# Eight-column clearings behind the scatters of the last groups and blocks, and five groups finished two blocks later

## The chip, the core and the metric

The kernel runs on one NeuronCore of a Trainium2 chip. The metric is the time of one execution on the device in microseconds (us); the time of a kernel is the median of its runs. An execution has five engines that work side by side: TensorE (PE, matmuls), VectorE (DVE), ScalarE (ACT), GpSimd (POOL) and SyncE (SP), each with its own queue of instructions, tied together by semaphores. In this kernel SP issues nearly all plain transfers, and POOL issues the scatters, which write rows to places in DRAM that a table names.

## The reference

4096 rows (tokens) of 128 numbers go through two stages, each wrapped as `x + layernorm(f(layernorm(x)))`. The first `f` is causal linear attention with 16 heads. The second is a mixture of eight experts, each row sent to its best two, beside one shared expert:

```
shared = new_gelu(xf @ Wfc_s + bfc_s) @ Wproj_s + bproj_s
probs = jax.nn.softmax(xf @ Wr, axis=-1)
topk_p, topk_i = jax.lax.top_k(probs, TOP_K)          # 2 of 8
topk_p = topk_p / jnp.sum(topk_p, axis=-1, keepdims=True)
...
for e in range(N_EXPERTS):
    h = new_gelu(xf @ Wfc[e] + bfc[e]) @ Wproj[e] + bproj[e]
    routed = routed + h * gate[:, e:e + 1]
return (shared + routed)
```

All inputs and outputs are float32 with rows of 128; an expert has 512 hidden units.

## The kernel before

The rows are cut into eight groups of 512 (`NS` = 8, four tiles of 128 rows each). A first phase works the attention and the shared expert group by group and routes each row: POOL scatters a group's rows into one list per expert in DRAM (`scatters`, L708; eight scatters a group, one for each tile and choice). The second phase works the lists in `NB` = 39 blocks of 256 rows. It has a loop on each engine:

- SP (`load_block`, `load_weights`, `load_rows`) loads a block's packed weights into one of six buffers (`NBUF` = 6), after `blk_yr` says that the block six before has been read, and then the block's rows.
- PE (`rows_turned`, `first_layer`, `second_layer`) turns the rows of block b, does the first layer of block b-1 (36 matmuls, L1524 to L1526) and the second layer of block b-2 (16 matmuls, L1551, semaphore `blk_mm2`). The second layer waits for the gelu, the gelu for `blk_fc`, which PE raises behind a first layer.
- ACT rounds weights and rows (L1134, L1138), and applies the gelu (L1154).
- DVE takes the remainders (L2125, L2128) and moves the second layer's result to SBUF (`yb`, L2157; it waits for `blk_mm2` and for the scatter of the block six before).
- POOL (`scatter_block`, L831) writes the block's 256 result rows to their places in `results`, as two scatters (c = 0 and 1). The two groups of rows that are routed last (eight scatters each) go through the same queue: the last of group 6's stand behind block 1.

**The clearings.** `still()` (L693) is a POOL instruction that writes zeros to a tile `spare` that nobody reads. In the kernel before it covers 128 x 384 numbers, and stands behind the last four scatters of one group, behind every scatter of the last two, behind both scatters of blocks 0 to 11, and behind the first scatter only of blocks 12 to 26; from block 27 on there is none. With 59 clearings, POOL's order is fixed by the program.

**Finishing a group.** When all blocks that can hold a group's rows have been scattered (`READY`), SP reads the group's results back (`results_in`, 512 KB; `Y_AFTER` says after which block). DVE multiplies by the gates and adds (`gated`, L2072; `GATED_AT`, `MOMENTS_AT`) and takes the moments, POOL takes the roots of two groups at a time (`roots`; `ROOTS_AFTER`), ACT normalizes (`final_norm`, L1170; `NORM_AT`), DVE adds the residual (`normed`, L2102; `NORMED_AT`), and SP stores the group (`store`). These tables place each of these steps behind the work of a block. Behind the loops stand the rest of the groups, the stores and the last group, whose results SP reads (`y_part`, L532) once every scatter has landed.

Of the kernel before, what the change touches and what calls it, by code (L numbers as in the profile page):

```python
# [15 lines left out]
P = 128  # L16
# [25 lines left out]
def sandwich_kernel(nc, x, w_qkv, b_qkv, w_out, b_out, wfc_s, bfc_s, wproj_s, bproj_s, wr, wfc, bfc, wproj,  # L42
# [7 lines left out]
    NB = PAIRS // BLK + NE - 1  # L50
# [11 lines left out]
    NBUF = 6  # L62
# [6 lines left out]
    LATE_SEGS = NS * NE + 1  # L69
    READY = [max(EARLY + NE, 2 * STEP * (g + 1) // BLK + NE - 1) for g in range(NS)]  # L70
    assert READY[NS - 1] == NB
    Y_AFTER = {26: 0, 27: 1, 28: 2, 30: 3, 34: 4, 38: 5}
    SHARED_FROM = 24

    lists = nc.dram_tensor("expert_lists", [NE * LIST + SPARE * BLK, ROW], F32).ap()
# [3 lines left out]
    with ExitStack() as ctx:  # L79
# [158 lines left out]


        ON_PE = 2  # L240
        spare = sb("spare", [P, 3 * P])
        diag = vr[:].rearrange("p e t -> p (e t)")[:, 0:2 * ON_PE * P].rearrange("p (t k d) -> p t k d", t=ON_PE, k=2)
        HALVED = 3

# [303 lines left out]
        def _(pool):  # L548
# [131 lines left out]
                       channel_multiplier=1).then_inc(s["pads_ready"], 1)  # L680

            AT_END = 4
            PAIRED = 27
            SINGLE = 2 * NBUF

            stills = [0]

# [131 lines left out]
            def scatter_block(b, n, turn):  # L819
                if isinstance(b, int) and b == 2:  # L820
                    scatters(NS + 1, 0, 2 * TILES)
                last = isinstance(b, int) and b >= NB - HALVED
                if last:
                    pool.wait_ge(s["half_yr"], b + 1 - NB + HALVED)
                else:
                    pool.wait_ge(s["blk_yr"], b + 1)
                    alone(pool)
                for c in range(2):
                    if last and c:
                        pool.wait_ge(s["blk_yr"], b + 1)  # L830
                    g.indirect_dma_start(  # L831
                        out=results,
                        out_offset=bass.IndirectOffsetOnAxis(ap=yrow[n][:, c], axis=0),
                        in_=yb[n][:, c, :], in_offset=None).then_inc(blk_scat[n], 16)
                    if b < SINGLE or b < PAIRED and c == 0:
                        still()

            def roots(pair):
# [11 lines left out]
                pool.wait_ge(s["fin_pow"], 2 * pair + 2)  # L850
                g.tensor_tensor(shift[:, at], neg_mean[:, at], rstd[:, at], ALU.mult).then_inc(s["fin_shift"], 1)

            ROOTS_AFTER = {26: 0, 30: 1}

            def step(b, n, turn):

# [7 lines left out]
        def _(act):  # L864
# [301 lines left out]
            def final_norm(g, tiles=range(TILES)):  # L1166
# [5 lines left out]
                if TILES - 1 in tiles:  # L1172
                    ins.then_inc(s["fin_n"], 1)

            NORM_AT = {32: (0, (0, 1)), 33: (0, (2, 3)), 34: (1, (0, 1)), 35: (1, (2, 3)), 37: (2, (0, 1)),
                       38: (2, (2, 3)), 39: (3, (0, 1, 2, 3))}

            ENDS_FROM = 5

# [438 lines left out]
        def _(dve):  # L1618
# [487 lines left out]
                dve.wait_ge(s["fin_n"], g + 1)  # L2106
                residual(g)

            GATED_AT = {25: 0, 27: 1, 29: 2, 31: 3, 33: 4, 37: 5}
            MOMENTS_AT = {26: 0, 28: 1, 30: 2, 32: 3, 34: 4, 38: 5}  # L2110
            NORMED_AT = {35: 0, 36: 1}

            def step(b, n, turn):

# [65 lines left out]

            gated(6, 1)
            moments(6)
            normed(2)
            normed(3)

# [56 lines left out]
```

## Time and profile before

| | |
|---|---|
| median of 3 runs | 385.13 us (382.33 to 385.97) |
| the profiled execution | 381.27 us, its span 379.4 us |
| PE busy | 336.1 us, 89% of the span |
| POOL busy | 290.6 us (77%); scatters L831 78 x 1009 ns, L708 64 x 1005 ns, clearings L693 59 x 436 ns |
| DVE, ACT busy | 288.4 us, 256.8 us |
| granted PE clock | mean 0.967 of full speed |

The profile is of one execution. A busy share is an average over stages with different limits, so the argument has to be made in the stretch in question. Starts of matmuls are recorded, their ends are modelled; "remote" as the reason for a wait means that the profile has no event that explains it.

### The profile page before, as it was taken

To read this page: it belongs to the slowest core of one execution; us is meant where nothing else is said; L and a number is where in the kernel's file an instruction comes from. 1 tells how busy PE (TensorE), PEld (TensorE's weight loads), DVE (VectorE), ACT (ScalarE), POOL (GpSimd) and SP (SyncE) were. 2 spreads that over 40 slices of the span, in tenths; PEclk is the share of its full clock that TensorE was granted. 3 is DMA by queue.
4 is the path that set the end of the run, shared out by engine and by line. 5 is a ranking of instruction groups with operands and counts; after the bars stand their busy time and mean duration, and the time that the engine had idled before them with its cause. 6 is when DMAs were issued, how large, how long until landed. Compare 5 with 4: busy or idle time off the path is not lost.

```text
span 379.4 us, 8176 instructions
## 1 busy us (share of the span) xinstructions
PE 336.1 (89%) x2497; PEld 291.0 (77%) x2497; DVE 288.4 (76%) x688; ACT 256.8 (68%) x692; POOL 290.6 (77%) x393
## 2 busy tenths in 40 slices
PE   7869896999899898998799998999998699989891
PEld 3538485797786867877598898889997699989871
DVE  4998999799899999899966467745543359687667
ACT  3958874896896887867426884466552477587674
POOL 8778799478888687888778888888888667776640
PEclk9979997999999999999999999999998899999997
DMA  6576766566382606125059569979874589987417
GB/s 188 164 208 182 179 167 125 114 199 156 113 225 76 177 31 182 48 90 156 30 168 278 147 181 268 263 239 282 263 244 147 165 267 383 314 243 246 125 56 204
DMA packets 53522, 69.18 MB, mean 182 GB/s; under 512 B 6365, under 2 KB 37386, under 8 KB 53482
## 3 DMA queue, kind: packets, MB, share of 16 engines
q1 hardware_dynamic: 47556, 58.58, 54.5%
q0 software_dynamic: 4544, 9.35, 7.3%
q10 hardware_dynamic: 1382, 0.79, 0.8%
q8 instruction: 16, 0.26, 0.3%
q14 instruction: 24, 0.20, 0.2%
HBM read 40.06 MB, written 18.15 MB: 153 GB/s over the span
## 4 chain that ended last, share of the span: by engine, by line
PE 29%; DVE 16%; issue 8%; ACT 7%; POOL 7%; another core or an unknown queue 2%; DVEq 0%; ACTq 0%; POOLq 0%
PE bO L1551 8%; PE bS L1551 6%; POOL expert_lists L708 4%; DVE KV L1702 3%; ACT hs L1154 2%; PE bV L1526 2%; PE bV L1524 2%; PE bV L1525 2%; DVE KV L1693 1%; DVE Z L1710 1%; PE bO L1335 1%; DVE X L1625 1%; PE bA L1524 1%; DVE w_lo L2125 1%
## 5 line engine op out<-in xcount | busy, mean ns | idle before, releaser
L831 POOL DMA_INDIRECT expert_results<-yb,yrow x78 | 78.7, 1009 | 29.5 <-issue 19.3
L708 POOL DMA_INDIRECT expert_lists<-rows,pos x64 | 64.3, 1005 | 19.4 <-issue 17.2
L1702 DVE TENSOR_TENSOR_SCAN KV<-bS,KV 128x1024 f32<-128x1024 bf16 x32 | 72.7, 2276 | 0.3
L1335 PEld LDWEIGHTS bO<-wout_rot,Z 128*128 128x128 f32 x512 | 60.6, 192 | 8.4 <-POOL Z L790 5.1
L1335 PE MATMUL bO<-wout_rot,Z 128*128 128x128 f32 x512 | 63.2, 277 | 2.1 <-POOL Z L790 1.8
L2149 DVE COPY yrow<-xb 128x2 int32<-128x2 int32 x24 | 7.7, 321 | 42.3 <-remote 18.7
L1154 ACT ACTIVATE hs<-bV,KV 128x256 f32<-128x256 f32 x56 | 22.0, 477 | 18.9 <-PE bV L1526 10.4
L1551 PE MATMUL bO<-KV,hs 128*128 128x128 f32 x232 | 30.5, 286 | 3.7 <-ACT hs L1154 2.3
L1551 PEld LDWEIGHTS bO<-KV,hs 128*128 128x128 f32 x232 | 28.5, 199 | 5.1 <-ACT hs L1154 3.2
L1305 PE MATMUL bA<-w2s_sb,hs 128*128 128x128 f32 x224 | 28.8, 277 | 0.0
L734 POOL TENSOR_TENSOR KV<-shared,vr 128x1024 f32<-128x1024 f32 x10 | 23.6, 2363 | 5.7 <-ACT shared L995 5.4
L1305 PEld LDWEIGHTS bA<-w2s_sb,hs 128*128 128x128 f32 x224 | 27.3, 193 | 0.2
L1524 PE MATMUL bV<-x_lo,w_hi 128*128 128x256 f32 x80 | 24.2, 302 | 3.3 <-DVE x_lo L2128 1.6
L1551 PE MATMUL bS<-Z,hs 128*128 128x128 f32 x192 | 24.1, 280 | 2.5 <-ACT hs L1154 2.5
L1693 DVE TENSOR_TENSOR KV<-bV,vr 128x1024 f32<-128x1024 f32 x22 | 25.9, 1201 | 0.4 <-DMA vr<-vr 0.4
L693 POOL MEMSET spare<- 128x384 f32 x59 | 25.8, 436 | 0.0
L1551 PEld LDWEIGHTS bS<-Z,hs 128*128 128x128 f32 x192 | 23.0, 196 | 2.7 <-ACT hs L1154 2.7
L881 ACT ACTIVATE rows<-X,shift,rstd 128x128 f32<-128x128 f32 x32 | 13.2, 482 | 16.3 <-POOL shift L626 16.3
L1154 ACT ACTIVATE hs<-bA,Z 128x256 f32<-128x256 f32 x24 | 10.1, 473 | 19.7 <-PE bV L1526 7.3
L1526 PE MATMUL bV<-x_hi,w_lo 128*128 128x256 f32 x80 | 22.3, 279 | 0.2 <-issue 0.2
L1525 PE MATMUL bV<-x_hi,w_hi 128*128 128x256 f32 x80 | 22.3, 279 | 0.0
L1710 DVE TENSOR_TENSOR Z<-KV,bV 128x1024 f32<-128x1024 f32 (+1 forms) x22 | 21.1, 1010 | 0.0
(370 smaller groups left out, 995.9 us busy)
## 6 DMA issues: line engine op xcount, KB each, us to landing
KV<-packed_weights SPq DMA_DIRECT2D x21, 578.0 KB
Z<-packed_weights SPq DMA_DIRECT2D x18, 578.0 KB
xb<-expert_lists SPq DMA_DIRECT2D x39, 129.0 KB
vr<-vr SPq DMA_DIRECT2D x16, 224.0 KB, 2.5
shared<-expert_results SPq DMA_DIRECT2D x7, 512.0 KB
vr<-vr SPq DMA_DIRECT2D x16, 192.0 KB
vr<-vr SPq DMA_DIRECT2D x16, 160.0 KB
vr<-vr SPq DMA_DIRECT2D x16, 128.0 KB
```

Of the source, the lines that this page charges most:

```text
L693: g.memset(spare[:], 0.0).then_inc(s["stilled"], 1)
L708: g.indirect_dma_start(out=lists, out_offset=bass.IndirectOffsetOnAxis(ap=pos[:, m:m + 1], axis=0), in_=rows[:, m // TILES, m % TILES, :], ...
L831: g.indirect_dma_start(out=results, out_offset=bass.IndirectOffsetOnAxis(ap=yrow[n][:, c], axis=0), in_=yb[n][:, c, :], in_offset=None).th ...
L1154: ins = a.activation(hb[m % 2][:, c], blk_h[m % 2][c // 2][:, (c % 2) * BLK:(c % 2 + 1) * BLK], ACT.Gelu_apprx_tanh, bias=wb[m][:, B1_AT + ...
L1305: ins = t.matmul(bA[:, j * D:(j + 1) * D], hs[:, c, j * P:(j + 1) * P], w2s_sb[:, c], start=False, stop=True, skip_group_check=True)
L1335: ins = t.matmul(bO[:, j * D:(j + 1) * D], Z[:, d, j * P:(j + 1) * P], wout_rot[:, d], start=False, stop=True, skip_group_check=True)
L1524: t.matmul(h, w[0], x_lo[m % 2][:], start=True, stop=False)
L1525: t.matmul(h, w[0], x_hi[m % 2][:], start=False, stop=False)
L1526: ins = t.matmul(h, w[1], x_hi[m % 2][:], start=False, stop=True)
L1551: ins = t.matmul(bank_y[:, r * D:(r + 1) * D], hb[m % 2][:, c, r * P:(r + 1) * P], wb[m][:, HID + c * D:HID + (c + 1) * D], start=(c == 0 ...
L1693: v.tensor_tensor(KV[:, 2 * pair:2 * pair + 2], bK[:].unsqueeze(1).broadcast_to([P, 2, STEP]), vr[:, 2 * pair:2 * pair + 2], ALU.mult).the ...
L1702: v.tensor_tensor_scan(w, ps_keep, w, 0.0, ALU.mult, ALU.add).then_inc(s["kv_sum"], 1)
```

## The change

There are two. First, `spare` is 8 columns wide instead of 384, and a clearing now stands behind both scatters of every block up to 35 (all but the last three); the two constants that said where clearings thin out and end are gone. The scatters of the groups keep theirs. There are 92 clearings (20 behind scatters of groups and 72 behind those of blocks) where there were 59. Second, groups 0 to 3 are read back two or three blocks later, and the gating, the moments, the roots and the norms of groups 0 to 4 (gating and moments of 0 to 4, norms of 0 to 2) stand two blocks later, or one; the residual of group 1 stands behind the loop.

```
-    Y_AFTER = {26: 0, 27: 1, 28: 2, 30: 3, 34: 4, 38: 5}
+    Y_AFTER = {29: 0, 30: 1, 31: 2, 32: 3, 34: 4, 38: 5}
-        spare = sb("spare", [P, 3 * P])
+        spare = sb("spare", [P, 8])
-            PAIRED = 27
-            SINGLE = 2 * NBUF
-                    if b < SINGLE or b < PAIRED and c == 0:
+                    if b < NB - HALVED:
                         still()
-            ROOTS_AFTER = {26: 0, 30: 1}
+            ROOTS_AFTER = {28: 0, 32: 1}
-            NORM_AT = {32: (0, (0, 1)), 33: (0, (2, 3)), 34: (1, (0, 1)), 35: (1, (2, 3)), 37: (2, (0, 1)),
-                       38: (2, (2, 3)), 39: (3, (0, 1, 2, 3))}
+            NORM_AT = {34: (0, (0, 1)), 35: (0, (2, 3)), 36: (1, (0, 1)), 37: (1, (2, 3)), 38: (2, (0, 1, 2, 3)),
+                       39: (3, (0, 1, 2, 3))}
-            GATED_AT = {25: 0, 27: 1, 29: 2, 31: 3, 33: 4, 37: 5}
-            MOMENTS_AT = {26: 0, 28: 1, 30: 2, 32: 3, 34: 4, 38: 5}
-            NORMED_AT = {35: 0, 36: 1}
+            GATED_AT = {27: 0, 29: 1, 31: 2, 33: 3, 35: 4, 37: 5}
+            MOMENTS_AT = {28: 0, 30: 1, 32: 2, 34: 3, 36: 4, 38: 5}
+            NORMED_AT = {37: 0}
             moments(6)
+            normed(1)
             normed(2)
```

On POOL, at the scatters of blocks 12 to 14, the order before is this (L831 is a block's scatter, two to a block, from the buffer `yb` of the block's number modulo 6; L693 is the clearing):

```order
L831 DMA expert_results<-yb0,yrow0 12032x128
L693 MEMSET spare 128x384
L831 DMA expert_results<-yb0,yrow0 12032x128
L831 DMA expert_results<-yb1,yrow1 12032x128
L693 MEMSET spare 128x384
L831 DMA expert_results<-yb1,yrow1 12032x128
L831 DMA expert_results<-yb2,yrow2 12032x128
L693 MEMSET spare 128x384
```

The same place after the change:

```order
L829 DMA expert_results<-yb0,yrow0 12032x128
L691 MEMSET spare 128x8
L829 DMA expert_results<-yb0,yrow0 12032x128
L691 MEMSET spare 128x8
L829 DMA expert_results<-yb1,yrow1 12032x128
L691 MEMSET spare 128x8
L829 DMA expert_results<-yb1,yrow1 12032x128
L691 MEMSET spare 128x8
L829 DMA expert_results<-yb2,yrow2 12032x128
L691 MEMSET spare 128x8
```

Each scatter has its clearing now, and the clearing is 8 wide; before, from block 12 on, a block's second scatter and the next block's first stood side by side.

On ACT, from behind the gelu in block 36's step, the order before is this (L1154 is the gelu of a block, L1170 the norm of two tiles or four, L1134, L1138 and L1142 a block's roundings and row numbers):

```order
L1134 ACTIVATE w_hi<-KV 128x512
L1138 ACTIVATE x_hi<-bH 128x256
L1142 ACTIVATE yrow<-xb 128x2
L1154 ACTIVATE hs<-bV,KV 128x256 x4
L1170 ACTIVATE SH<-SH,shift,rstd 128x128 x2
L1134 ACTIVATE w_hi<-KV 128x512
L1138 ACTIVATE x_hi<-bT 128x256
L1142 ACTIVATE yrow<-xb 128x2
L1154 ACTIVATE hs<-bA,KV 128x256 x2
L1154 ACTIVATE hs<-bB,KV 128x256 x2
L1170 ACTIVATE SH<-SH,shift,rstd 128x128 x2
```

The same place after the change:

```order
L1168 ACTIVATE SH<-SH,shift,rstd 128x128 x2
L1132 ACTIVATE w_hi<-KV 128x512
L1136 ACTIVATE x_hi<-bH 128x256
L1140 ACTIVATE yrow<-xb 128x2
L1152 ACTIVATE hs<-bV,KV 128x256 x4
L1168 ACTIVATE SH<-SH,shift,rstd 128x128 x2
L1132 ACTIVATE w_hi<-KV 128x512
L1136 ACTIVATE x_hi<-bT 128x256
L1140 ACTIVATE yrow<-xb 128x2
L1152 ACTIVATE hs<-bA,KV 128x256 x2
L1152 ACTIVATE hs<-bB,KV 128x256 x2
L1168 ACTIVATE SH<-SH,shift,rstd 128x128 x4
```

Block 36's step has gained the norm of two tiles, and block 38's now has four tiles instead of two ahead of the last block's gelu; the steps of blocks 32 and 33, further ahead, have lost theirs.

## Rows read from the trace of the kernel before

**Rows 1.** The page's costliest groups: scatters of blocks, and clearings.
```profile
L831 POOL DMA_INDIRECT expert_results<-yb,yrow x78 | 78.7, 1009 | 29.5 <-issue 19.3
...
L693 POOL MEMSET spare<- 128x384 f32 x59 | 25.8, 436 | 0.0
```

**Rows 2.** Windows: stretch, length, each engine's busy us, granted clock, DMA share, GB/s.
```profile
257.00:277.00 20.00, 20.00 (x178) 20.00 (x177) 10.92 (x32) 12.22 (x30) 18.02 (x25) 1.00 0.89 269
280.00:298.00 18.00, 13.62 (x94) 12.22 (x92) 4.22 (x12) 5.29 (x14) 14.69 (x19) 0.91 0.55 169
```

**Rows 3.** Timeline of PE: start, us; second layers of blocks 17, 18, 21, 22, 35.
```profile
276.86 1.95 PE L1551 MATMUL bS<-Z,hs 128*128 128x128 f32 x16
...
280.28 1.95 PE L1551 MATMUL bO<-KV,hs 128*128 128x128 f32 x16
...
298.50 1.27 PE L1551 MATMUL bS<-Z,hs 128*128 128x128 f32 x9 [2.48 <-ACT hs L1154]
...
303.62 1.95 PE L1551 MATMUL bO<-Z,hs 128*128 128x128 f32 x16
...
350.79 1.95 PE L1551 MATMUL bS<-Z,hs 128*128 128x128 f32 x16
```

**Rows 4.** Timeline of POOL: start, us, in brackets the idle time before it.
```profile
223.87 0.97 POOL L831 DMA_INDIRECT expert_results<-yb,yrow  x1 [0.16 <-issue]
...
278.00 0.96 POOL L831 DMA_INDIRECT expert_results<-yb,yrow  x1 [0.30 <-issue]
...
299.70 0.97 POOL L831 DMA_INDIRECT expert_results<-yb,yrow  x1 [2.19 <-DVE yb L2157]
```

**Rows 5.** Timeline of all engines: who waits between 283 and 292.
```profile
283.58 0.28 PE L1526 MATMUL bV<-x_hi,w_lo 128*128 128x256 f32 x1
...
287.50 1.57 ACT L1154 ACTIVATE hs<-bV,KV 128x256 f32<-128x256 f32 x4 [4.93 <-remote]
...
291.13 0.17 DVE L2149 COPY yrow<-xb 128x2 int32<-128x2 int32 x1 [5.56 <-remote]
```

**Rows 6.** The same in the first phase: the last of four scatters, then ACT.
```profile
94.05 0.96 POOL L708 DMA_INDIRECT expert_lists<-rows,pos  x1 [0.31 <-issue]
...
95.83 0.60 ACT L1030 ACTIVATE SH<-bA 128x512 f32<-128x512 f32 x1 [3.13 <-remote]
```

**Rows 7.** The same behind block 27, where no clearing stands.
```profile
330.25 0.96 POOL L831 DMA_INDIRECT expert_results<-yb,yrow  x1 [0.31 <-issue]
...
331.80 0.42 DVE L2157 TENSOR_TENSOR yb<-bS,Z 128x256 f32<-128x256 f32 x1 [2.36 <-remote]
...
335.98 0.96 POOL L831 DMA_INDIRECT expert_results<-yb,yrow  x1 [0.60 <-issue]
...
336.63 0.47 ACT L1154 ACTIVATE hs<-bV,KV 128x256 f32<-128x256 f32 x1 [1.21 <-issue]
```

**Rows 8.** POOL's instructions by form: a clearing of the setup, busy us, mean ns.
```profile
L580 POOL MEMSET eps<- 1x1 bf16 x3 | 0.3, 94 | 0.0
```

**Rows 9.** Timelines of ACT and POOL: last sum and roots before the last groups' rows.
```profile
209.98 0.19 ACT L934 ACTIVATION_READ_ACCUMULATOR shared<-X,neg_mean_scaled 128x1 f32 x1
...
210.94 0.22 POOL L622 TENSOR_TENSOR ve<-sq,ln_eps 128x4 f32<-128x4 f32 x1
```

**Rows 10.** The page: SP's reads of a group's results, KB each.
```profile
shared<-expert_results SPq DMA_DIRECT2D x7, 512.0 KB
```

**Rows 11.** Timelines of the tail: ACT ahead of the last gelu, SP, DVE.
```profile
358.65 0.89 ACT L1170 ACTIVATE SH<-SH,shift,rstd 128x128 f32<-128x128 f32 x2
...
367.79 2.22 SPq L532 DMA_DIRECT2D shared<-expert_results  x4
369.32 0.23 DVE L2187 RECIPROCAL rstd<-ve 128x12 f32<-128x12 f32 x1 [1.75 <-ACT ve L1195]
```

**Rows 12.** Timeline of DVE: the results of blocks 3 and 10.
```profile
227.33 0.61 DVE L2157 TENSOR_TENSOR yb<-bS,Z 128x256 f32<-128x256 f32 x1
...
255.84 0.42 DVE L2157 TENSOR_TENSOR yb<-bO,Z 128x256 f32<-128x256 f32 x1
```

## The prediction

> **What bounds the kernel now.** The page's costliest groups come first, for the size of what is changed: 78 scatters of blocks at 1009 ns and 59 clearings at 436 ns [rows 1]. POOL is busy for 77% of the span and PE for 89%, so what the clearings are worth has to be read where PE waits. The windows show two kinds of stretch [rows 2]. In 257 to 277, with a wide clearing at every block, PE is busy for 20.00 of 20 us. In 280 to 298 it is busy for 13.62 of 18, its granted clock falls from 1.00 to 0.91, and DVE and ACT do less than half as much (4.22 and 5.29 us): nobody works much, so there something is late for all of them.
>
> The timeline of PE gives the size. Second layers start at 276.86 and 280.28, a pace of 3.42 us a block; blocks 18 to 22 go from 280.28 to 303.62, 23.34 us where four blocks at that pace take 13.68 [rows 3]. So 9.7 us are lost there. From 22 to 35 it is 47.17 us for thirteen blocks, against 44.46 at that pace: 2.7 us more.
>
> The timeline of POOL shows what is particular to the place. In the kernel before, the clearings thin out at block 12, and POOL, which is behind with its scatters, works them off without a pause. A scatter that stands beside another starts 0.30 us behind it [rows 4], where a clearing of 0.44 with its issue makes the gap about 0.60. POOL has caught up at 299.70, where for the first time it waits for a result (`yb`). That is also where PE resumes. The timeline of all engines says how they are held: PE has finished a first layer at 283.58 + 0.28 = 283.86, but ACT, which waits for nothing else, starts its gelu at 287.50 after 4.93 us of a wait that is put down to "remote" (no event explains it), and DVE comes back only at 291.13 after 5.56 us [rows 5]. A run of four scatters in the first phase did it too: the last one ends at 94.05 + 0.96 = 95.01 and ACT, idle for 3.13 us, goes on at 95.83 [rows 6]. And behind block 27, where there is no clearing: scatter over at 331.21, DVE's sum at 331.80 after 2.36 us [rows 7]. I read this as one mechanism: while POOL issues scatters close together, news from PE reaches the others late, mostly in a bunch after the last of them. It costs 9.7 us in one run of scatters, and pieces of a microsecond or two behind block 27.
>
> **The change, part by part.**
>
> *The clearings behind blocks 12 to 35.* 33 more than before, on an engine that is waited for only in its long run. If a clearing of 8 columns does what the wide one does, the stretch of blocks 18 to 22 runs like 257 to 277 [rows 2], and its 9.7 us go (−9.7). Of the 2.7 behind block 22, some belongs to other causes, since also with wide clearings not every wait is gone; I take −2.0.
>
> *The width.* A clearing of 1 x 1 took 94 ns [rows 8] and the wide one, 384 columns, 436 ns [rows 1]; 128 x 8 has to lie between. By columns it is next to the first, and I take 0.11. So a clearing falls from 0.44 to 0.11, and the period of POOL's run from about 1.6 us to 0.97 + 0.11 + 0.17 = 1.25 a scatter. POOL is not what PE waits for in the second phase as long as it has six buffers in hand, so that is worth nothing by itself there. At the passage between the phases it is on the path: five clearings stand in POOL's run ahead of the roots of the last group, which start at 210.94, and 5 x 0.33 = 1.7 us would be the most. But ACT hands over the last sum at 209.98 + 0.19 = 210.17 [rows 9], so at most 0.77 can be gained; I take −0.5 (bounds 0 and −0.8).
>
> *Finishing later.* The reads of groups 0 to 3, 512 KB each [rows 10], now come behind blocks 29 to 32 in succession, ahead of the loads of blocks some six further on; a late load there has that lead to hide in, so 0 (if the lead were gone, a read would cost its own time, at most some 2 us). The gating, moments and roots only change places within the loops, equal work, 0. ACT's norms are not hidden: the norm of two tiles at 358.65 takes 0.89 us ahead of the last gelus [rows 11], about 0.77 of it not overlapped with its neighbours, and there is one such pair more in block 36's step and one more in block 38's, where ACT is next to PE in the chain that ends last: +1.5 (bounds 0, if ACT waits there anyway, and +1.8). DVE's residual of group 1 moves behind the loop, 0.66 us into idle time of 1.75 us that it has before 369.32 [rows 11]: 0. SP's store of group 1 moves with it, ahead of the last reads of results; four of those take 2.22 us to issue [rows 11], 0.55 each, and a store of one or two issues delays them by 0.55 to 1.1: +0.8.
>
> *The sum*: −9.7 − 2.0 − 0.5 + 1.5 + 0.8 = −9.9, made against the profiled execution's own 381.27, which gives 371.4. That execution is 3.9 us below the median of 385.13, so on the median it is 375.2: 375.
>
> **What speaks against it.** One row weighs on the step that all of this rests on. With a clearing 8 wide the gap between two scatters is 0.11 + 0.17 = 0.28 us. That is no longer than the 0.30 that stands between two scatters with nothing between them [rows 4], and those are the ones that hold PE's news back. The pause that is known to let it through is 0.60 long. Behind block 27 there is even a row for a pause of 0.60 without a clearing: the scatter at 335.98 stands 0.60 behind its neighbour, and ACT's gelu at 336.63 waited for nothing but its issue [rows 7]. What acts may therefore be the length of the pause, not that something else was executed.
>
> The Trainium skill bears on this in the GPSIMD Engine Reference, section 2.1 (Instruction dispatch): consecutive Pool instructions are no barrier between the engine's eight cores; each starts on the next instruction as soon as its own share is done. In DMA: Bandwidth & Descriptors, section SWDGE vs HWDGE vs iDMA, it says that two of those cores compute a scatter's descriptors and write them to rings in SBUF. By these two, a narrow clearing is for the two cores in question only a very short break and no fence, which speaks for the length of the pause; no row here shows the cores apart. By that rule the time would be the one that rival B gives from rows; if the clearing as an instruction is what lets the news through, it is the one above.
>
> **The rivals.**
>
> *B, the narrow clearing does not work like the wide one (slower).* Its place is the whole run of scatters from the last groups on. POOL's gaps there are then 0.28 instead of 0.60, from about 203 on, and the mechanism that now costs 9.7 us in 280 to 298 holds in the early blocks. The price of a block in it: 280.28 to 298.50 for three blocks, 6.07 us instead of 3.42, +2.65 [rows 3]. How long it would last: POOL's first scatter of a block is at 223.87 [rows 4]; eleven clearings ahead of it are 0.33 shorter, so it starts near 220.2; up to block 10 there are 30 scatters at 1.24, which end at 257.4, and block 10's result is there at 255.84 [rows 12]. So POOL catches up near 257 rather than near 299.70. In the 37 us up to there some 6 blocks would be done at 6.07, and the loss is 6 x 2.65 = 16, less what this stretch loses already: results of blocks 3 to 10 come from 227.33 to 255.84 [rows 12], 4.07 us a block, 0.65 x 7 = 4.6. That leaves +11.3, and +1 for the last groups. Against it the late stall goes, −9.7, and the tail and the passage stay as above, +2.3 − 0.5 (nothing off for the lags behind block 27, which B leaves). Sum +4.4: 385.7 of its own, 390 on the median. At half the price of a block the stretch costs 8 − 4.6 = 3.4 and the sum is −3.5, 382 on the median. I take 387, nearer to the whole price, and 380 to 396 as its bounds. It decides between 0.30 (holds) and 0.60 (passes) of gap.
>
> *C, the stall goes, but the end gives it back.* With POOL and PE earlier by 10 us, reads, norms and loads of blocks 29 to 38 meet in a stretch where SP moves a load and a read of 512 KB in every block. If the six-block lead is used up there and the norms are all on the path, some 6 us of the 12 come back: 381 on the median.
>
> *D, the scatters are not the cause.* Then the 9.7 us come from something else in 280 to 298 (transfers have a share of 0.55 there against 0.89 ahead of it [rows 2], so not from their mass), the change moves it elsewhere, and the tail's +2.3 remain: 385 to 387.5. The three places [rows 5 to 7] have nothing else in common than scatters side by side, so I hold it for unlikely.
>
> **How the numbers follow.** The forecast 0.5: every stretch with clearings between the scatters keeps PE running, and the change gives that to the places that had none. B 0.3: its gap speaks for it and only a size of clearing, not its presence, is changed in the first half. C 0.1, D 0.1. The forecast alone spans 370 to 379: the tail at its bounds (−2.3, or +1 and the read's 2), the run of the medians 382 to 386 around its own. To leave out 2 in 10 the range has to reach through C and D and into the lower half of B: 368 to 390. A difference of 1%, 3.9 us, is about what a measurement of this kernel can tell from no change. Faster by more than 1% (below 381.3): the forecast nearly whole, half of C, a little of B: 0.58. Slower by more than 1% (above 389.0): the upper part of B, 0.20 with some of D. The rest, 0.22, lies within.
>
> **What the next profile would show.** Right: clearings at 100 to 150 ns, no wait of over 3 us on "remote" on ACT or DVE, PE's second layers 3.4 to 3.5 us apart from block 3 to 35, its granted clock near 1.00 in 280 to 298, POOL's first wait for `yb` near block 10, at about 257. If B is right, that wait still comes near there, but PE is busy for only two thirds of 220 to 257, with ACT and DVE on "remote" waits. The steps of the tail show as the starts of ACT's norms around block 38, and as the issue of the last reads behind a store. What would make it wrong: the gap of 0.28 acting like 0.30 (B), or a price of the late stall that does not vanish when its scatters are set apart.

## The result, and the profile after

The changed kernel takes 394.08 us (median of 4, 393.25 to 396.69), the kernel before 385.29 in the same job (382.33 to 385.97). The ratio is 1.027, with an interval of 1.023 to 1.031: slower by 2.7%. The profiled execution took 394.43, its span is 392.6 us against 379.4. I had forecast 375, and given rival B, which ends slower, a chance of 0.3.

Where the 13.2 us of span went is read off the starts of PE's second layers (L1549 of the changed kernel is L1551 of the one before):

| from, to | before, us | after, us | difference |
|---|---|---|---|
| start to block 0 | 211.67 | 213.19 | +1.5 |
| block 0 to 7 | 29.75 | 46.82 | +17.1 |
| block 7 to 17 | 35.44 | 36.64 | +1.2 |
| block 17 to 22 | 26.76 | 18.81 | −8.0 |
| block 22 to 35 | 47.17 | 48.41 | +1.2 |
| block 35 to the end | 28.6 | 28.7 | +0.1 |

The stall behind block 18 [rows 2, 3] is gone almost in full, and twice as much has come up in the first seven blocks. Windows of the changed kernel (the stretch, its length, then busy us of PE, PEld, DVE, ACT and POOL, granted clock, share of the DMA engines, GB/s):

```profile
203.00:220.00 17.00, 14.59 (x129) 14.00 (x130) 8.72 (x28) 11.63 (x33) 11.83 (x22) 1.00 0.56 176
220.00:260.00 40.00, 24.52 (x186) 22.97 (x185) 16.05 (x72) 13.42 (x29) 25.23 (x47) 0.83 0.49 134
280.00:298.00 18.00, 16.42 (x145) 16.22 (x144) 8.74 (x24) 8.34 (x21) 11.30 (x22) 1.00 0.80 243
```

The same windows of the kernel before, of which only the last is in [rows 2]:

```profile
203.00:220.00 17.00, 15.48 (x138) 14.97 (x138) 9.61 (x38) 11.95 (x33) 15.33 (x22) 1.00 0.66 198
220.00:260.00 40.00, 36.84 (x330) 35.57 (x328) 26.01 (x91) 23.72 (x54) 35.86 (x52) 1.00 0.88 245
```

In 220 to 260 PE is busy for 24.5 of 40 us instead of 36.8, and its granted clock falls to 0.83. In 280 to 298 it is busy for 16.4 where it was for 13.6. The timelines of the changed kernel show who waits, and for what, from 217 to 231:

```profile
218.91 0.96 PE L1351 MATMUL bS<-wr_sb,xt 128*128 128x8 f32 x8
...
221.27 0.28 PE L1524 MATMUL bB<-x_hi,w_lo 128*128 128x256 f32 x1
229.37 0.21 PE L1359 MATMUL bS<-chosen,before 128*128 128x32 bf16 x1 [7.82 <-DVE chosen L1748]
...
217.08 0.42 DVE L2126 TENSOR_TENSOR x_lo<-bH,x_hi 128x256 fp32r<-128x256 f32 x1
227.09 0.19 DVE L1713 COPY lg<-bS 128x32 f32<-128x32 f32 x1 [9.59 <-remote]
...
219.59 0.66 ACT L1132 ACTIVATE w_hi<-Z 128x512 fp32r<-128x512 f32 x1
227.26 0.84 ACT L1152 ACTIVATE hs<-bA,Z 128x256 f32<-128x256 f32 x2 [7.02 <-remote]
```

PE has finished its first layer at 221.27 + 0.28 = 221.55; the gelu that waits for it starts at 227.26, 5.7 us later. DVE waits from 217.50 on for the router's product of PE, which PE finishes at 219.87, and takes it up at 227.09, 7.2 us later. POOL's timeline has a run of nine scatters at the same time, the last of which ends at 225.62:

```profile
213.83 1.41 POOL L706 DMA_INDIRECT expert_lists<-rows,pos  x1 [0.17 <-issue]
215.24 0.12 POOL L691 MEMSET spare<- 128x8 f32 x1
...
223.38 0.97 POOL L829 DMA_INDIRECT expert_results<-yb,yrow  x1 [0.18 <-issue]
224.34 0.13 POOL L691 MEMSET spare<- 128x8 f32 x1
224.66 0.96 POOL L829 DMA_INDIRECT expert_results<-yb,yrow  x1 [0.19 <-issue]
225.62 0.12 POOL L691 MEMSET spare<- 128x8 f32 x1
230.51 0.97 POOL L829 DMA_INDIRECT expert_results<-yb,yrow  x1 [4.77 <-DVE yb L2155]
```

A scatter, a clearing of 0.12 and 0.18 of issue: a period of 1.27 us and a pause of 0.31, with the news released behind the last of the run. That is the pattern of [rows 4, 5] at another place. The hold is not there from the first scatter on: the run begins at 213.83, and ACT still starts a gelu at 218.16, 1.3 us behind the first layer that it waits for, with other work in between. A second run of twelve, 230.51 to 245.45, is two scatters of block 1, the eight of the last group (group 7, and not group 6 as the description of the kernel before says) and two of block 2. DVE goes on behind it at 247.87, after 12.31 us on "remote"; the second layer that it waits for had ended at 235.24 + 1.95 = 237.19.

PE itself is held as well, which the word "news" does not cover. In the second layer below the program has a wait only ahead of the first of 16 matmuls, and yet they come one or a few at a time, and the profile has no event for the gaps ("issue"):

```profile
235.24 1.95 PE L1549 MATMUL bS<-Z,hs 128*128 128x128 f32 x16
...
242.24 0.77 PE L1549 MATMUL bO<-Z,hs 128*128 128x128 f32 x3 [2.78 <-issue]
244.89 0.37 PE L1549 MATMUL bO<-Z,hs 128*128 128x128 f32 x1 [1.88 <-issue]
246.35 0.37 PE L1549 MATMUL bO<-Z,hs 128*128 128x128 f32 x1 [1.08 <-issue]
247.75 2.51 PE L1549 MATMUL bO<-Z,hs 128*128 128x128 f32 x11 [1.03 <-issue]
```

The traces therefore do not tell a signal that comes late from engines that are themselves held up. Below, "held news" is the name of the pattern and not of a shown mechanism.

### The profile page after: what moved, and what is told of

The parts are those of the page before. It is cut to its first block, busy times and chain, and to the rows that moved or that the text cites. A ratio compares the mean times of both kernels' runs of the same rounds, so it can differ in the third digit from the quotient of the medians.

```text
span 392.6 us, 8202 instructions
## 1 busy us (share of the span) xinstructions
PE 335.2 (85%) x2490; PEld 291.4 (74%) x2497; DVE 288.7 (74%) x688; ACT 256.5 (65%) x692; POOL 278.0 (71%) x426
## 4 chain that ended last, share of the span: by engine, by line
PE 36%; POOL 15%; ACT 15%; issue 11%; DVE 8%; another core or an unknown queue 7%; SPq 3%; DMA 3%; POOLq 1%; DVEq 0%; ACTq 0%
PE bS L1549 7%; PE bO L1333 7%; PE bO L1549 6%; POOL expert_lists L706 3%; ACT hs L1152 3%; ACT hs L1023 2%; POOL Z L788 2%; PE bV L1522 2%; DVE SH L2070 2%; ACT shared L894 2%; POOL Z L793 2%; PE bV L1523 2%; PE bV L1524 2%; DMA shared<-expert_results 1%
## 5 line engine op out<-in xcount | busy, mean ns | idle before, releaser
L829 POOL DMA_INDIRECT expert_results<-yb,yrow x78 | 79.8, 1023 | 52.8 <-DVE yb L2155 33.4
L2147 DVE COPY yrow<-xb 128x2 int32<-128x2 int32 x24 | 4.5, 189 | 45.4 <-remote 22.1
L1549 PE MATMUL bO<-KV,hs 128*128 128x128 f32 x232 | 31.0, 289 | 4.6 <-ACT hs L1152 4.4
L1549 PEld LDWEIGHTS bO<-KV,hs 128*128 128x128 f32 x232 | 28.8, 201 | 6.0 <-ACT hs L1152 6.0
L732 POOL TENSOR_TENSOR KV<-shared,vr 128x1024 f32<-128x1024 f32 x10 | 23.6, 2362 | 5.7 <-ACT shared L993 4.6
L1549 PE MATMUL bS<-Z,hs 128*128 128x128 f32 x192 | 23.5, 275 | 0.2 <-ACT hs L1152 0.2
L879 ACT ACTIVATE rows<-X,shift,rstd 128x128 f32<-128x128 f32 x32 | 13.2, 482 | 15.4 <-POOL shift L626 15.3
L1549 PEld LDWEIGHTS bS<-Z,hs 128*128 128x128 f32 x192 | 22.4, 192 | 0.4 <-ACT hs L1152 0.4
L1708 DVE TENSOR_TENSOR Z<-KV,bV 128x1024 f32<-128x1024 f32 (+1 forms) x22 | 21.1, 1011 | 0.0
L1549 PE MATMUL bO<-Z,hs 128*128 128x128 f32 x96 | 13.8, 294 | 6.8 <-issue 6.8
```

The lines of the kernel that those rows point to most:

```text
L732: g.tensor_tensor(KV[:, 2 * pair:2 * pair + 2], keys.unsqueeze(1).broadcast_to([P, 2, STEP]), vr[:, 2 * pair:2 * pair + 2], ALU.mult).then ...
L829: g.indirect_dma_start(out=results, out_offset=bass.IndirectOffsetOnAxis(ap=yrow[n][:, c], axis=0), in_=yb[n][:, c, :], in_offset=None).th ...
L1549: ins = t.matmul(bank_y[:, r * D:(r + 1) * D], hb[m % 2][:, c, r * P:(r + 1) * P], wb[m][:, HID + c * D:HID + (c + 1) * D], start=(c == 0 ...
```

## The experiments

A job is one session on one chip, in which some kernels and the kernel before are run. All runs stand against the kernel before in the same job. **That kernel itself turned out to take 374 us in three of the eight jobs and 380 to 385 in five**, and the two kinds of job differ in the traces. I call them free and held. This is the table of all 18 runs, by job:

| job (chip) | before | kernel | median | ratio (interval) |
|---|---|---|---|---|
| 1 (4), free | 374.47 | e1 narrow alone | 365.51 | 0.975 (0.969 to 0.980) |
| | | e2 later alone | 369.50 | 0.987 (0.983 to 0.991) |
| | | e3 wide everywhere | 381.58 | 1.019 (1.015 to 1.023) |
| | | e4 none | 366.96 | 0.981 (0.974 to 0.987) |
| 2 (8), held | 384.72 | e5 changed | 396.15 | 1.030 (1.028 to 1.033) |
| | | e6 before, one run | 383.21 | |
| 3 (6), free | 374.12 | e7 narrow alone | 363.93 | 0.972 (0.969 to 0.976) |
| | | e8 later alone | 368.27 | 0.984 (0.982 to 0.987) |
| | | e9 none | 364.92 | 0.975 (0.970 to 0.980) |
| | | e10 three narrow | 397.03 | 1.060 (1.057 to 1.063) |
| 4 (6), held | 383.71 | e11 changed | 394.38 | 1.026 (1.018 to 1.034) |
| | | e12 narrow alone | 396.18 | 1.029 (1.020 to 1.038) |
| | | e13 wide, later | 379.83 | 0.991 (0.988 to 0.994) |
| 5 (9), held | 384.07 | e14 three narrow | 398.44 | 1.038 (1.033 to 1.044) |
| | | e15 changed | 398.38 | 1.034 (1.029 to 1.040) |
| 6 (7), free | 374.21 | e16 two narrow, later | 381.35 | 1.021 (1.016 to 1.026) |
| | | e17 none | 364.33 | 0.973 (0.969 to 0.976) |
| 7 (14), held | 380.11 | e18 changed | 391.68 | 1.029 (1.022 to 1.037) |

The job of the result above (held) is the eighth.

**The two parts alone, wide clearings everywhere, and none (job 1).** The edits, each on the kernel before: e1 takes over the clearings of the change, e2 its tables, and e3 and e4 are (shortened)

```
e3:  -  if b < SINGLE or b < PAIRED and c == 0:
     +  if b < NB - HALVED:                      (spare stays 128 x 384)
e4:  -  if in_passage(i, first): still()
     -  if b < SINGLE or b < PAIRED and c == 0: still()
```

> The kernel before with the changed clearings alone: 8 columns wide, behind every scatter up to block 35; the groups are finished where they were before. Theory (the pause between scatters decides, and 0.31 us is too short): the loss sits here, 220 to 257 runs with PE busy for two thirds only, and the time is that of the changed kernel less the tail's share of at most 2 us: 391 to 394 us. Rival (the later finishing costs the 9 us, the clearings are neutral or help): 376 to 386 us.

> The kernel before with the later finishing alone: clearings as before, 384 wide and thinned out from block 12. Theory: the stretch 203 to 300 is as before, with its stall of about 9.7 us in 280 to 298, and the tail gives +2.3 (two norms ahead of the last gelus 1.5, a store ahead of the last reads 0.8): 386 to 389 us. Rival (the later finishing is what made it slower): 392 us or more. A third, from the reads of results being better placed: 381 to 384.

> The kernel before with its clearings of 384 columns, but behind both scatters of every block up to 35; the groups finished as before. Theory (a pause of 0.6 us between scatters lets the news of PE through): the stall of 280 to 298 goes (-9.7) and the lags behind block 27 in part (-2), none of the rest changes: 372 to 377 us. Rival (the late stall has another cause, or POOL with the longer period falls behind and becomes what is waited for): 382 to 388 us.

> The kernel before without any clearing, so scatters stand 0.30 us apart throughout; the groups finished as before. Theory (only the length of the pause counts): like the narrow clearings, 391 to 394 us, with the same two waits of about 10 us of DVE in 216 to 248. Rival (a clearing of any width does something by being there): the stalls of the early blocks are longer than with narrow ones, 397 us or more.

Neither theory nor rival had this, but for e3, where the rival (POOL falls behind) came close. Narrow clearings alone gained 2.5%, none at all gained 1.9%, the later finishing gained 1.3%, wide ones everywhere lost 1.9%. And the kernel before took 374.5. The trace of e2, which has the clearings of the kernel before, shows why these four can't be held against the verdict. On POOL, bare scatters stand 0.30 apart from block 12 on as in [rows 4], and PE's second layers of blocks 18 to 21 come 3.41 to 3.42 us apart all the same:

```profile
275.96 0.95 POOL L831 DMA_INDIRECT expert_results<-yb,yrow  x1 [0.30 <-issue]
276.90 0.44 POOL L693 MEMSET spare<- 128x384 f32 x1
277.51 0.96 POOL L831 DMA_INDIRECT expert_results<-yb,yrow  x1 [0.17 <-DVE yb L2157]
278.78 0.95 POOL L831 DMA_INDIRECT expert_results<-yb,yrow  x1 [0.30 <-issue]
...
278.25 1.95 PE L1551 MATMUL bO<-KV,hs 128*128 128x128 f32 x16
281.66 1.95 PE L1551 MATMUL bS<-KV,hs 128*128 128x128 f32 x16
285.08 1.95 PE L1551 MATMUL bO<-KV,hs 128*128 128x128 f32 x16
288.50 1.95 PE L1551 MATMUL bS<-Z,hs 128*128 128x128 f32 x16
```

No wait in these four traces is put down to "remote". There was no held news in this job, so what is left to see is the price of POOL's lateness. The waits of SP in e3 (engine and line, what it waited for: us in total, times, longest):

```profile
SPq L508 <- DMA expert_results<-yb,yrow: 36.1, 3, 13.9
```

and of PE:

```profile
PE bH L1377 <- DMA xb<-expert_lists: 10.0, 2, 9.7
```

Behind the loads of block 26 SP waits for the scatters up to block 20 (`READY` of group 0 is 21) before it reads group 0's results back; the loads of later blocks stand behind it in its queue, and PE runs out of blocks for 9.7 us. In e1, with the shorter period, the waits of L508 are 20.7 us, in e2, with the later read, 8.4. So in a free job both parts of the change relieve the same wait, and wide clearings only cost. Narrow ones cost nothing that can be told from none at all (0.975 against 0.981). There is no trace of the kernel before from a free job, so how much of either gain comes out of this wait is argued and not shown.

**The changed kernel and the one before again (job 2).**

> The changed kernel itself, once more. In the four runs ahead of this one the kernel before took 374.5 us, not 385.3, and no trace of them has a wait on remote on ACT or DVE, not even the one without any clearing, where the trace of the changed kernel has 34 us of them on ACT and 35 on DVE. Theory (the held back news of PE depends on the chip that the kernel runs on, and where it is absent the narrow clearings cost nothing and the later finishing gains): if this runs on a chip that does not hold it back, 361 to 366 us against 374.5, with no remote waits; on one that does, 393 to 396 against 385. Rival (narrow clearings and later finishing together make the stalls, on any chip): 2 to 3% slower than the kernel before here too, with DVE waits of about 10 us in 216 to 248.

> The kernel before itself, for a trace on this chip. Theory: where it takes 374 to 375 us, its trace has no waits on remote, and 280 to 298 has PE busy throughout; where it takes 385, the stall of rows 3 to 5 is there again. Rival (the 10 us between 385 and 374 come from another stretch, in the first phase): the stretch 280 to 298 looks as before either way.

3.0% slower, as in the first comparison, with 40.3 us of gelus waiting on "remote". The kernel before's own trace again has such waits (27.0 us on gelus, 29.0 on DVE's L2149), but not at the same place: blocks 14 to 18 take 21.8 us, from 268.74 to 290.57, 8.2 more than four blocks at the steady pace. Most of it is lost where on POOL the bare pauses of 0.30 us begin, as in [rows 4], with the scatters of block 12 at 275.6; ahead of that, at 0.60 us, the waits on "remote" in the second phase are of 3.4 us at most. I took this for two kinds of chip.

**Four kernels once more (job 3).** e10 has three narrow clearings where the changed kernel has one (shortened):

```
-    g.memset(spare[:], 0.0).then_inc(s["stilled"], 1)
+    for _ in range(3):
+        if stills[0]: pool.wait_ge(s["stilled"], stills[0])
+        stills[0] += 1
+        g.memset(spare[:], 0.0).then_inc(s["stilled"], 1)      (spare 128 x 8)
```

> The changed clearings alone (as in the run e1_narrow_alone), to have them on a chip where the kernel before takes 385 and its trace has waits on remote (a holding chip, below). So far: on one chip the kernel before took 374.5 and nothing was held back, on another 384.7 and the changed kernel was 3% slower. Theory: on a holding chip the narrow clearings carry the whole loss, 393 to 398 against 385; on the other kind 365 against 374.5 again. Rival (the later finishing shares in the loss on a holding chip): 386 to 391.

> The later finishing alone. Theory: on a holding chip it gains what it gained on the other kind, 1.3%, or nothing, since its reads do not wait so long for POOL: 380 to 386; it does not lose. Rival (it shares in the loss): 388 to 392. On a chip of the other kind 369 against 374.5 again.

> No clearing at all. Theory (length of the pause): on a holding chip as slow as with narrow ones or slower, 394 to 400, with waits on remote of 10 us; on the other kind 367. Rival (clearings of any width do nothing for the held news, which then has to do with DVE or the transfers): as the kernel before, 385.

> Three clearings of 8 columns in a row where the changed kernel has one (each waits for the one ahead of it), so that the pause between scatters is some 0.7 us without anything wide being written; groups finished as before. Theory (only the length of the pause counts): on a holding chip few waits on remote in 216 to 260, and a time like that of the kernel before or below, 378 to 387. Rival (it is the width of what is written that counts): like the narrow ones, 393 to 398. On a chip of the other kind the longer period costs some of what the narrow ones gain: 366 to 375.

A free job. The first three repeat job 1 (−2.8, −1.6, −2.5%). e10 was off by far: 397 instead of 366 to 375. Three narrow clearings occupy as much time as a wide one, but the pause is as long as the wide one's (0.59 to 0.60 us) only between scatters of a group and within a block. Ahead of the first scatter of a block it is 1.08 to 1.13 us, so a block takes POOL 3.6 us where it takes 3.1 in e3. POOL's idle time ahead of block scatters that is put down to issue is 25.8 us, in e3 it is 13.1. Why the issue takes longer there is not shown. POOL falls further behind, and SP waits 43.0 us at L508, 16.3 of them at a time.

**Changed, narrow alone, and wide with the later finishing (job 4).**

> The changed kernel. The chips come in two kinds so far: a holding one (before 385, changed +3.0%, waits on remote) and two free ones (before 374, none). Theory: on a free chip both gains add, -2.7% for the narrow clearings and at most -1.4% for the later finishing: 358 to 364 against 374, no waits on remote; on a holding chip 394 to 397 against 385. Rival (the two parts together lose on either kind): 380 or more on a free chip.

> The changed clearings alone. Theory: on a holding chip they carry the whole loss, 393 to 398; on a free one 364 to 366 again. Rival (the later finishing has a part in the loss, since with news held back every step behind the loop comes late): 386 to 391 on a holding chip.

> Clearings of 384 columns behind both scatters of every block up to 35, and the later finishing of the change. Theory: the wide clearings keep the pause at 0.6 us, so that a holding chip holds nothing back behind block 11 either, and the later finishing takes away the wait of SP for POOL's late scatters, 36 us in the run with wide ones everywhere: 368 to 376 on a holding chip, 368 to 374 on a free one. Rival (POOL's period of 1.57 us is too long, and the wait only moves to the last groups): 378 to 384 on either.

This job ran on the chip of job 3 and was held, so it is not the chip. It settles which part costs in a held job: narrow clearings alone are 2.9% slower, both parts together 2.6%, and the later finishing adds nothing that can be told from zero. The cleanest comparison within one job is e11 with e13: they differ in the width of `spare` alone, 8 columns or 384, and take 394.38 and 379.83 us. The longest wait on "remote" is 12.6 us in e11 and 3.5 in e13. The same kernel file, narrow alone, took 363.9 in job 3 and 396.2 here, and its two traces are the clearest pair of the study. Windows of e7 (free):

```profile
220.00:260.00 40.00, 37.95 (x329) 37.29 (x328) 24.60 (x82) 23.86 (x56) 34.47 (x61) 1.00 0.98 276
```

and of e12 (held):

```profile
220.00:260.00 40.00, 26.00 (x190) 24.42 (x190) 16.12 (x72) 13.83 (x30) 25.23 (x46) 0.79 0.51 146
```

Of 40 us PE works for 38 in the one and for 26 in the other. The waits of e7, the longest groups of DVE and ACT in the second phase:

```profile
DVE yrow L2147 <- PE bS L1549: 16.6, 10, 2.0
ACT hs L1152 <- PE bB L1524: 20.2, 18, 2.6
```

The same of e12, with waits of up to 12.2 and 9.7 us:

```profile
DVE yrow L2147 <- remote: 18.6, 3, 12.2
DVE lg L1713 <- remote: 12.4, 2, 8.9
ACT hs L1152 <- remote: 33.8, 7, 9.7
ACT SH L1028 <- remote: 9.1, 3, 4.5
```

e13 is the forecast as it should have been made: wide clearings behind every scatter. Its PE shows no stall behind block 18, second layers of blocks 17, 18, 21 and 22:

```profile
281.99 2.05 PE L1549 MATMUL bS<-Z,hs 128*128 128x128 f32 x16 [0.19 <-ACT hs L1152]
285.51 1.95 PE L1549 MATMUL bO<-KV,hs 128*128 128x128 f32 x16
...
295.76 1.95 PE L1549 MATMUL bS<-Z,hs 128*128 128x128 f32 x16
299.18 1.05 PE L1549 MATMUL bO<-Z,hs 128*128 128x128 f32 x8
```

17.19 us for five blocks where the kernel before took 26.76. Yet it is only 0.9% faster, not the 2 to 4% expected. Its waits on "remote" are short in the second phase (at most 2.9 us on DVE, 2.6 on ACT's gelus) but many, 24.5 us on gelus alone. Blocks 5 to 17 take 49.68 us, where e3, which has the same clearings in a free job, takes 45.58: a pause of 0.6 us takes away the long waits of a held job and not all of them. The time lies in the rival's range, 378 to 384, but not for the rival's reason: SP waits only 6.3 us at L508.

**Is it the length of the pause or the width? (job 5)**

> Three clearings of 8 columns behind every scatter up to block 35 (a pause of 0.59 us, as with the wide one), groups finished as before. In a job that was free of held news this took 397 us against 374, since POOL's late scatters hold up SP's reads and loads. In a job that holds news back (before 384): theory (the length of the pause counts): no wait on remote of over 4 us in 216 to 260, where the narrow one has 9 to 12; the time is still near 397 for the other reason. Rival (the width of what is written counts): waits of 9 to 12 us as with one narrow clearing.

> The changed kernel. Theory: in a free job (before 374) both parts' gains, 358 to 364 us and no waits on remote; in one that holds 394 to 397 against 384. Rival: the parts together lose in a free job too, 380 or more.

A held job, with e15 3.4% slower. e14 has clearings as narrow as e15's, but a pause of 0.59 to 0.60 us between the scatters of a group and within a block, as with the wide one; ahead of a block's first scatter it is 1.07 us and more. POOL in e14, at a group's scatters and ahead of a block's:

```profile
217.60 0.96 POOL L707 DMA_INDIRECT expert_lists<-rows,pos  x1
218.56 0.45 POOL L692 MEMSET spare<- 128x8 f32 x3
...
242.89 0.44 POOL L692 MEMSET spare<- 128x8 f32 x3
243.98 0.96 POOL L830 DMA_INDIRECT expert_results<-yb,yrow  x1 [0.65 <-issue]
```

Windows of e14 (held), and then of e10, the same kernel in a free job:

```profile
220.00:260.00 40.00, 34.89 (x308) 33.57 (x305) 22.66 (x78) 22.88 (x51) 29.64 (x93) 1.00 0.88 229
```

```profile
220.00:260.00 40.00, 34.74 (x313) 33.66 (x312) 22.75 (x89) 22.43 (x50) 30.35 (x90) 1.00 0.84 225
```

PE is busy for 34.9 and 34.7 us: with this pause the held job costs nothing there, where with one narrow clearing it cost 12 of 40 us. The eight scatters of the last group, 230.5 to 242.9, stand 0.59 to 0.60 us apart throughout, so the longer pauses ahead of blocks are not what does it there; e15, in the same job and with 0.31 us, waits 12.2 us in that stretch. DVE's only wait of over 3 us on "remote" is 3.5 us, at 200, in a run of scatters of the first phase that has no clearings. Not everything is on time: ACT's gelus have 21.1 us of waits that are put down to issue, in 16 pieces of at most 2.9 us, which e10 has not; they do not reach PE. The medians do not speak against it, though 397 us in a free job is the wait of SP and hides much: three narrow took 398.4 held and 397.0 free, narrow alone 396.2 and 363.9, the kernel before 384 and 374. One wide clearing (e13) and three narrow ones (e14) both take the long waits away, one narrow one (e11, e12) does not: neither the width nor the number of instructions is common to the first two, only the pause. So it is the pause between scatters that lets the news through, and not the width of what is written. The time is as bad as in job 3 for the other reason (SP waits 42.7 us at L508).

**Two narrow with the later finishing, and none (job 6).** e16 is the changed kernel with `range(2)` in the loop above.

> Two clearings of 8 columns where the changed kernel has one, all else as changed: a pause of about 0.45 us and a period of 1.42. In a job that holds news back: theory (the pause decides, somewhere between 0.31 and 0.59, and the later finishing makes room for POOL's lateness): if 0.45 is long enough, no waits of over 4 us on remote in 216 to 260 and 366 to 376 us against 384; if not, 388 to 396 with such waits. In a free job 360 to 366 against 374.

> No clearing at all, groups finished as before: scatters 0.30 us apart. Theory (a narrow clearing is as good as none, since the pause is 0.31 with it): in a job that holds news back as slow as narrow ones alone, 394 to 398 against 384, with waits of 9 to 12 us on remote in 216 to 250. Rival (being there counts for something): longer waits, 400 or more. In a free job 365 to 367 again.

A free job, so the question of a pause between 0.31 and 0.59 was not answered. The pause of e16 was 0.43 to 0.44 us within a block and 0.92 ahead of one, not 0.45 throughout. e17 gained 2.7%, as before. e16 lost 2.1% where I had expected a gain: two clearings a scatter make POOL late even with the later reads (SP waits 23.6 us at L508, DVE 17.2 for scatters of the block six before).

**The changed kernel, once more (job 7).**

> The changed kernel, for the last time. Theory: in a job that is free of held news (before 374) the narrow clearings' -2.7% and something of the later finishing's -1.5%: 358 to 364 us, and no wait on remote; in one that holds (before 384) 394 to 398. Rival (the parts hinder each other in a free job): 366 to 374 or more.

Held, 2.9% slower, 12.1 us at once on "remote" in DVE; its 391.7 us are below the 394 to 398 expected, as the kernel before's 380.1 are below 384. So the changed kernel was never run in a free job; whether its two gains add there is open.

## Why the prediction was wrong

- **What bounds the kernel now** was read rightly. Where scatters stand 0.6 us apart (e13) the stall behind block 18 is gone in a held job; in a free one the same bare scatters do no harm (e2). It takes both: scatters close together and a held job. That the state of the job counts was in no rival.
- **The term of −9.7 us** came true in size and not by its mechanism. Blocks 18 to 22 took 9.2 us less (17 to 22: 8.0), but the narrow clearings did not let the news through; POOL was no longer behind. Block 18's first scatter comes 3.9 us behind its second layer, which starts at 301.30, and POOL waits for the result ahead of it; before it came 11.9 us behind, at 292.15 in a long run:

```profile
305.24 0.97 POOL L829 DMA_INDIRECT expert_results<-yb,yrow  x1 [1.75 <-DVE yb L2155]
```

  Rival B had the late stall go too. The −2.0 for the lags behind block 22 was +1.2.
- **The step that failed** is the one that all of it rests on, "if a clearing of 8 columns does what the wide one does". It doesn't in a held job (e11 against e13). Its size was right (124 ns measured in e1, 0.11 forecast), and with it the pause: 0.12 + 0.18 = 0.31 us. The row that spoke against it was there, 0.30 between bare scatters [rows 4], and a second one [rows 7] said that a pause of 0.60 without a clearing lets the news pass. I gave a chance of 0.5 to the reading without a row of its own, and 0.3 to the one that had two.
- **Rival B** is what happened, in its place and by one of its marks (PE at less than two thirds in 220 to 260, on "remote" waits elsewhere). The other mark, POOL's first wait for `yb` near 257, missed: it came at 230.51. The price was too low: blocks 0 to 7 took 17.1 us more and blocks 0 to 10 16.0, for which I had 11.3. A block in a held run did not cost 6.07 us but up to 12.9, from block 1 at 217.10 to block 2 at 230.00. The early stretch has runs of nine and twelve scatters at 0.31 us, since groups' scatters go in front of blocks' two, where in the stall of [rows 3] pauses of 0.30 and 0.60 alternate. That this is why a block cost more there was not tested.
- **The passage**, forecast −0.5, became +1.5. ACT's last sum, which had been ready 0.77 us ahead [rows 9], is now what POOL waits for, and ACT's own work ahead of it had waits on "remote". POOL's timeline and ACT's waits in the changed kernel:

```profile
211.78 0.19 POOL L622 TENSOR_TENSOR ve<-sq,ln_eps 128x4 f32<-128x4 f32 x1 [3.37 <-ACT shared L932]
...
ACT SH L1028 <- remote: 8.1, 2, 4.6
```
- **The tail**, forecast +2.3, was +0.1 between block 35 and the end. The norms stand where the order said, four tiles for 1.65 us at 369.41 and one pair at 365.95, ahead of the last gelus, and the last reads are issued behind one more store:

```profile
369.41 1.65 ACT L1168 ACTIVATE SH<-SH,shift,rstd 128x128 f32<-128x128 f32 x4
...
379.67 0.38 SPq L395 DMA_DIRECT2D out<-SH  x1
380.71 2.41 SPq L532 DMA_DIRECT2D shared<-expert_results  x4
```

  The store took 0.38 us to issue, not 0.55 to 1.1, and the reads come 16.8 us behind block 35's second layer where they came 17.0 behind it [rows 3, 11]. The two norms were hidden: ACT stood idle for 1.18 us behind them, ahead of the last gelus at 372.34. In free jobs the later finishing even gained 1.3 and 1.6%, probably by a term that I had put at 0: the reads no longer wait as long for POOL in front of SP's loads (8.4 us in e2; 20.7 in e1 and e4, which have the earlier reads).
- **Rule and rows.** The reading that I drew from the Trainium skill's two pages (GPSIMD Engine Reference, section 2.1, and DMA: Bandwidth & Descriptors, section SWDGE vs HWDGE vs iDMA), that a narrow clearing is no fence but only a short break, would have given the time of rival B. The runs agree with it as far as the length of the break goes: three narrow ones in a row do what one does not. No run shows the engine's cores apart, so the mechanism behind it is not shown.

What is shown, then: in a held job PE's work is taken up late, in waits of up to 12.6 us, while scatters stand 0.31 us apart, and in none above 3.5 us when they stand 0.59 apart (e11 against e13, e12 and e15 against e14). What is open: by what way scatters hold up the other engines, and what makes a job held. It is not the chip (chip 6 was both). All five held jobs had the changed kernel among theirs and none of the three free ones had it; in job 5 it was listed behind e14, whose trace already shows the holding. Whether that is cause or chance was not tested. Nor was no clearing at all run in a held job, nor the later finishing alone, nor a pause between 0.31 and 0.59.

The kernel to keep depends on that state. In held jobs e13 (wide everywhere, later finishing) is 0.9% faster than the kernel before and 3.7% faster than the changed one (379.83 against 394.38); in free jobs the best are the kernels with one narrow clearing or none, 2 to 3% faster than the kernel before, and e13 was not run there.

## What to carry to other kernels

When a filler instruction is made cheaper, ask first whether what it did was done by its cost: here the pause was the function, and the width only its price. Two rows of the trace (a bare gap that holds, a longer bare gap that passes) said so before any run; a reading that has rows behind it should not get a lower chance than one that has none. And compare a kernel's time only with runs of the same job: the same file took 364 and 396 us here.

## What the runs showed of the hardware

- The same kernel on the same chip has two behaviours from job to job: in one, ACT and DVE have no wait that is put down to "remote", also with scatters 0.30 us apart (e2, e4, e9, e17); in the other they have waits of up to 12.6 us (e11), and in the changed kernel DVE takes a result of PE up 10.7 us behind its end (237.19 to 247.87). The kernel before differs by 2.6% between them (374.2 and 384), one with narrow clearings by 9% (363.9 and 396.2).
- In held jobs PE also pauses within a layer, 1.0 to 1.9 us between matmuls that have no wait between them in the program (the changed kernel at 244 to 247; e12 at 240 and 241, 1.0 us). In the traces of free jobs no idle time of PE is put down to issue.
- In the held state a pause of 0.59 us between scatters of 0.96 us is enough to take waits of 9 to 12 us away; 0.31 us is not.
- On POOL three clearings of 128 x 8 with their waits occupy 0.44 us, as much as one of 128 x 384, and still cost more around them: the pause ahead of a block's first scatter is 1.08 us against 0.60, and the kernel takes 15 us more (e10 against e3, in two free jobs).
- Behind a long hold the granted clock of PE falls, so that a late signal is paid for twice. It is 0.74 to 0.83 of full speed in the windows of 20 us from 220 to 260 of the held traces with narrow clearings. In the changed kernel PE stands idle from 221.55 to 229.37; in windows of 1 us the clock is at 1.00 up to 226 and at the lower of its two levels, 0.50, from 227 to 233. A second layer that falls there takes 3.76 us instead of the 1.95 of the next one:

```profile
230.00 3.76 PE L1549 MATMUL bO<-KV,hs 128*128 128x128 f32 x16
```
